# Edge indicators made by ScalarE, a bias added a stage earlier by VectorE, and VectorE's indicators one visit ahead, in a two-layer graph kernel

## What is computed

```python
h = relu(_layernorm(x))
# first layer (attention over edges, then a feed-forward part)
q, k, v = split(layernorm(h) @ Wqkv + bqkv)              # 8 heads of 32
e = exp(scores(q[src], k[dst]) - m[dst])
agg = segment_sum(v[src] * e / s[dst], dst)
x1 = h + agg
x = x + x1 + gelu(layernorm(x1) @ W_in + b_in) @ W_out + b_out
h = relu(_layernorm(x))
# second layer (8 relations from 4 bases)
W = einsum('rb,bio->rio', comp, basis)
msgs = einsum('ni,rio->nro', h, W)[src, edge_type]
z = gelu(segment_sum(msgs, dst) + h @ loop_w + h_bias + h)
x = x + layernorm(z) * ln_gamma + ln_beta
```

## Time and profile before

| | us |
|---|---|
| median of three runs | 1415.9 (1413.2 to 1416.32) |
| the profiled execution's own time | 1415.08 |
| its span, first to last instruction | 1413.4 |

### The profile page before, as it was taken

One profiled execution on the slowest core, in us unless ns is written; L12 is line 12 of the kernel. 1 busy time (PEld: TensorE's weight loads), 2 busy tenths in 40 slices (PEclk: granted clock), 3 DMA queues, 4 the chain that ended last, 5 costly groups with the idle time before them and its releaser, 6 DMA issues.

```text
span 1413.4 us, 18069 instructions
## 1 busy us (share of the span) xinstructions
PE 1154.9 (82%) x5223; PEld 829.5 (59%) x5223; DVE 895.7 (63%) x2778; ACT 453.0 (32%) x1150; POOL 995.6 (70%) x1032
## 2 busy tenths in 40 slices
PE   4875859999999999999999989677676767767674
PEld 2443647777777777777777765345454444444453
DVE  5664668888888888888888863124543454345345
ACT  4644215444544454445444533100000000000000
POOL 2755778788878877888788610577777777777773
PEclk9988979999999999999999999777878787788877
DMA  7758787888788878887888621344444444444442
GB/s 245 209 164 297 241 230 208 251 270 262 234 249 264 262 236 241 255 250 227 238 256 252 195 75 60 113 117 127 130 127 133 124 134 124 134 126 128 130 125 86
DMA packets 143355, 266.14 MB, mean 188 GB/s; under 512 B 41674, under 2 KB 89908, under 8 KB 140310
## 3 DMA queue, kind: packets, MB, share of 16 engines
q0 software_dynamic: 59536, 167.31, 41.5%
q1 hardware_dynamic: 82758, 96.47, 20.8%
q10 hardware_dynamic: 960, 1.18, 0.3%
HBM read 199.25 MB, written 65.63 MB: 187 GB/s over the span
## 4 chain that ended last, share of the span: by engine, by line
PE 33%; POOL 26%; DVE 18%; issue 11%; DMA 3%; ACT 0%; POOLq 0%; DVEq 0%; SPq 0%
POOL arena L1279 23%; PE ps L1520 8%; PE ps L1543 6%; PE ps L1551 6%; PE ps L1569 4%; DVE arena L1811 3%; PE ps L1509 3%; DVE arena L1809 3%; DVE arena L1744 2%; POOL arena L1225 2%; PE ps L1681 2%; DMA arena<-h_all,typs 1%; DVE arena L671 1%; PE ps L1489 1%; DVE arena L673 1%
## 5 line engine op out<-in xcount | busy, mean ns | idle before, releaser
L1225 POOL DMA_INDIRECT arena<-qv_tab,srcs x392 | 407.5, 1040 | 127.4 <-issue 115.9
L1279 POOL DMA_INDIRECT arena<-h_all,typs x392 | 381.7, 974 | 159.8 <-issue 117.3
L1681 PE MATMUL ps<-arena 128*128 128x256 f32 x784 | 279.6, 494 | 150.5 <-DMA arena<-h_all,typs 147.1
L1681 PEld LDWEIGHTS ps<-arena 128*128 128x128 f32 x784 | 169.4, 236 | 240.2 <-DMA arena<-h_all,typs 199.5
L1520 PE MATMUL ps<-arena 128*128 128x264 f32 x784 | 213.9, 401 | 30.6 <-DVE arena L1744 30.5
L1569 PE MATMUL ps<-wrel,arena 128*128 128x512 f32 x400 | 189.7, 600 | 2.4 <-ACT arena L1344 2.4
L1520 PEld LDWEIGHTS ps<-arena 128*128 128x128 f32 x784 | 139.1, 193 | 69.1 <-DVE arena L1744 43.9
L1744 DVE TENSOR_TENSOR arena<-arena 128x512 f32<-128x512 f32 x196 | 136.9, 699 | 40.8 <-ACT arena L1312 40.8
L1509 PE MATMUL ps<-arena 128*128 128x264 bf16 x1032 | 142.3, 279 | 11.2 <-DMA arena<-k_tab 11.2
L1509 PEld LDWEIGHTS ps<-arena 128*128 128x128 bf16 x1032 | 125.3, 144 | 44.6 <-issue 35.4
L1869 DVE TENSOR_TENSOR arena<-ps,rowb 128x256 f32<-128x256 f32 x25 | 10.6, 425 | 218.8 <-PE ps L1669 218.8
(11 more groups left out here) (164 smaller groups left out, 1474.6 us busy)
## 6 DMA issues: line engine op xcount, KB each, us to landing
h_all<-arena SPq DMA_DIRECT2D x23, 1024.0 KB, 5.5
arena<-dst SPq DMA_DIRECT2D x49, 256.0 KB, 5.1
rel<-arena SPq DMA_DIRECT2D x77, 128.0 KB, 2.2
arena<-k_tab SPq DMA_DIRECT2D x49, 198.0 KB, 4.1
att<-arena POOLq DMA_DIRECT2D x49, 132.0 KB
qv_tab<-arena SPq DMA_DIRECT2D x25, 256.0 KB, 3.1
arena<-qv_tab,srcs POOLq DMA_INDIRECT x392, 4.2
arena<-h_all,typs POOLq DMA_INDIRECT x392, 2.8
```

The source lines that it names most:

```text
L1225: pool.indirect_dma_start(out=rowbuf[:, 2 * q + t % 2, 0:2 * D], out_offset=None, in_=qv_tab, in_offset=bass.IndirectOffsetOnAxis(ap=srcs[ ...
L1279: pool.indirect_dma_start(out=rows1[:, u * T + t, :], out_offset=None, in_=h_all[0:N * R, :], in_offset=bass.IndirectOffsetOnAxis(ap=typs[ ...
L1681: last = nc.tensor.matmul(ps[:, 6 + u, 0:D], ind1[:, u, t, :], rows1[:, u * T + t, :], start=(t == 0), stop=(v == 0 and t == T - 1))
```

## The change

1. `b_out` is loaded behind the last x chunk. In stage 1 VectorE waits for it once, ahead of the block loop, and adds it to a block of x right after each `take(b)`. GpSimd's `residual` in stage 2 then has one addition.
2. TensorE's `turn` in stage 2 is gone. VectorE computes, once, the negative offset of each edge's `dst` from its window's start (`ndl`). ScalarE takes, for each tile, the square of (column number + that offset), and of four tiles at once Relu(1 - 2 * square), which is 1 where the two agree and 0 elsewhere. The Squares stand among ScalarE's other work, in two groups of four per visit.
3. The bank that the turns used becomes a second bank for the sums (`bank_a`), so a visit's first sum waits for the copy of the sums two visits back.
4. In stage 3 VectorE builds the indicators of visit v + 1 during visit v, between `combine` and `finish` of the block that the visit before ended. The copy of h (`h1c`) and the bank of `loop_part` get a second buffer.

```diff
@@ SP, stage 1
                 load_x(5)
+                sp.dma_start(rowb[:, 0, :], b_out.partition_broadcast(P)).then_inc(bias_in, 16)
...
-                    if 19 <= b < 23:
-                        sp.dma_start(rowb[:, b - 19, :], (b_out, h_bias, gamma, beta)[b - 19].partition_broadcast(P)).then_inc(s_w2, 16)
+                    if 19 <= b < 22:
+                        sp.dma_start(rowb[:, b - 18, :], (h_bias, gamma, beta)[b - 19].partition_broadcast(P)).then_inc(s_w2, 16)
@@ VectorE, stage 1
                 dve.wait_ge(s_w, 64)
+                dve.wait_ge(bias_in, 16)
                 for b in range(NBLK):
                     c, p = b // CH + 2, b % CH
                     more = b < NBLK - CH
                     take(b)
+                    nc.vector.tensor_tensor(x_block(xs, b), x_block(xs, b), rowb[:, 0, :], ALU.add)
@@ stage 2, banks
-            TURN, AGG = 4, 5
+            def bank_a(v):
+                return 4 + v % 2
@@ GpSimd, residual
-                    nc.gpsimd.tensor_tensor(x_of(m), x_of(m), h_of(m), ALU.add).then_inc(x_added, 1)
-                    pool.wait_ge(x_added, m + 1)
-                    nc.gpsimd.tensor_tensor(x_of(m), x_of(m), rowb[:, 0, :], ALU.add).then_inc(x_ready, 1)
+                    nc.gpsimd.tensor_tensor(x_of(m), x_of(m), h_of(m), ALU.add).then_inc(x_ready, 1)
@@ ScalarE, stage 2
-                def indicators(v):
-                    act.wait_ge(turn_ready, v + 1)
+                def distances(v, half):
                     if v >= 2:
                         act.wait_ge(agg_done, PAIRS * (v - 1))
-                    for half in range(2):
-                        nc.scalar.activation(ind[:, v % 2, 4 * half:4 * half + 4, :],
-                                             ps[:, TURN, half * 2 * WIN:(half + 1) * 2 * WIN].bitcast(BF16).rearrange("p (t w) -> p t w", w=WIN),
-                                             ACT.Copy).then_inc(ind_ready, 1)
+                    for t in range(4 * half, 4 * half + 4):
+                        last = nc.scalar.activation(ind[:, v % 2, t, :], iotaj[:, :], ACT.Square, bias=ndl[:, v, t:t + 1])
+                    last.then_inc(squares, 1)
+
+                def indicators(v, half):
+                    act.wait_ge(squares, 2 * v + half + 1)
+                    i = ind[:, v % 2, 4 * half:4 * half + 4, :]
+                    nc.scalar.activation(i, i, ACT.Relu, bias=ones[:, :], scale=-2.0).then_inc(ind_ready, 1)
@@ ScalarE, odd visits (even ones alike)
                         weights(v, 2)
+                        distances(v + 1, 0)
                         weights(v, 3)
+                        indicators(v + 1, 0)
                         if out:
                             keep_messages(out - 1, 2)
-                        indicators(v + 1)
+                        distances(v + 1, 1)
+                        indicators(v + 1, 1)
                         weights(v + 1, 0)
@@ TensorE, stage 2 (the three calls of turn are gone)
-                    if j == 0 and v >= 1:
-                        pe.wait_ge(osum_ready, v)
+                    if j == 0 and v >= 2:
+                        pe.wait_ge(osum_ready, v - 1)
                     for t in (2 * j, 2 * j + 1):
-                        last = nc.tensor.matmul(ps[:, AGG, 0:AW], ind[:, v % 2, t, :], rowbuf[:, 2 * ring(v, j) + t % 2, D:2 * D + H],
+                        last = nc.tensor.matmul(ps[:, bank_a(v), 0:AW], ind[:, v % 2, t, :], rowbuf[:, 2 * ring(v, j) + t % 2, D:2 * D + H],
@@ VectorE, stage 2, once
+                nc.vector.memset(ones, 1.0).then_inc(offsets_ready, 1)
+                nc.vector.tensor_tensor(ndl, wst[:, :].unsqueeze(2).broadcast_to([128, G, T]),
+                                        dstf[:, :].rearrange("p (g t) -> p g t", t=T), ALU.subtract).then_inc(offsets_ready, 1)
@@ VectorE, stage 3
+                indicators(0)
                 for v in range(G):
-                    m = block_of(v)
+                    ended = block_of(v - 1) if v else None
+                    if ended is not None:
+                        loop_sum(ended)
+                        combine(ended)
                     if v - 1 in EARLY:
                         loop_sum(EARLY[v - 1])
-                    if m is not None:
-                        copy_h1(m)
-                    indicators(v)
-                    if v % 2 and v > FIRST:
-                        loop_sum(block_of(v - 1))
-                        if v in EARLY:
-                            copy_h1(EARLY[v])
-                        combine(block_of(v - 1))
-                        finish(block_of(v - 1))
+                    if v + 1 < G:
+                        if loop_of(v + 1) is not None:
+                            copy_h1(loop_of(v + 1))
+                        indicators(v + 1)
+                    if ended is not None:
+                        finish(ended)
```

More of the change, by code:

```diff
@@ L725, in program @@
             zero = cut([D])
+            ndl = cut([G, T])
+            ones = cut([1])
             kg = cut([2, KW])
@@ L756, in bank_m @@
                 if m == LASTM - 1 and c >= 2:
-                    return (TURN, AGG)[c - 2]
+                    return (5, 4)[c - 2]
                 if m < LASTM:
@@ L1001, in program @@
             cut = carve()
-            h1c = cut([D])
+            h1c = cut([2, D])
             h1T1 = cut([2, P])
@@ L1367, in _ @@
                 diagonals(1)
-                indicators(0)
+                act.wait_ge(offsets_ready, 2)
+                for half in range(2):
+                    distances(0, half)
+                    indicators(0, half)
                 for v in range(G):
                     hid, out, old = hid_of(v), out_of(v), before(v)
+                    more = v + 1 < G
                     if v == FIRST:
-                        act.wait_ge(s_w2, 16 * 10)
+                        act.wait_ge(s_w2, 16 * 9)
                     if v == 0:
@@ L1398, in _ @@
                         keep_h1(old)
+                    if more:
+                        distances(v + 1, 0)
                     weights(v, 2)
+                    if more:
+                        indicators(v + 1, 0)
                     if old is not None:
@@ L1404, in _ @@
                     weights(v, 3)
-                    if v + 1 < G:
-                        indicators(v + 1)
+                    if more:
+                        distances(v + 1, 1)
+                        indicators(v + 1, 1)
                         weights(v + 1, 0)
@@ L1481, in _ @@
                         pe.wait_ge(special_over, 2)
-                def turn(v):
-                    if v >= 1:
-                        pe.wait_ge(ind_ready, 2 * v)
-                    tiles = indT[:, v % 2, :].rearrange("p (e t) -> p t e", t=T)
-                    for t in range(T):
-                        last = nc.tensor.transpose(ps[:, TURN, t * WIN // 2:(t + 1) * WIN // 2].bitcast(BF16),
-                                                   tiles[:, t, :], identb[:, :])
-                    last.then_inc(turn_ready, 1)
                 def keys(v, j):
@@ L1582, in _ @@
                 keys(0, 0)
-                turn(0)
                 keys(0, 1)
@@ L1588, in _ @@
                     if v == FIRST:
-                        pe.wait_ge(s_w2, 16 * 10)
+                        pe.wait_ge(s_w2, 16 * 9)
                     if v + 1 < BY_PE:
@@ L1599, in _ @@
                             message(out - 1, 2)
-                        turn(v + 1)
                         add_up(v, 2)
@@ L1631, in _ @@
                 penult, last = LASTM + 1, LASTM + 2
+                pe.wait_ge(osum_ready, G - 1)
                 message(LASTM - 1, 2)
@@ L1668, in loop_part @@
                     for k in range(2):
-                        last = nc.tensor.matmul(ps[0:P, 1, 0:D], h1T1[:, k, :], wloop[:, k, :],
+                        last = nc.tensor.matmul(ps[0:P, 1 + nth(m) % 2, 0:D], h1T1[:, k, :], wloop[:, k, :],
                                                 start=(k == 0), stop=(k == 1))
@@ L1863, in copy_h1 @@
                     dve.wait_ge(h1_kept, m + 1)
[L1864 removed]
+                    nc.vector.tensor_copy(h1c[:, nth(m) % 2, :], hs[:, m * D:(m + 1) * D]).then_inc(h1c_ready, 1)
                 def loop_sum(m):
@@ L1868, in loop_sum @@
                     dve.wait_ge(loop_psum, nth(m) + 1)
-                    own.did(nc.vector.tensor_tensor(h_m, ps[0:P, 1, 0:D], rowb[:, 1, :], ALU.add))
+                    own.did(nc.vector.tensor_tensor(h_m, ps[0:P, 1 + nth(m) % 2, 0:D], rowb[:, 1, :], ALU.add))
                     own.did(nc.vector.tensor_tensor(xs[:, m * D:(m + 1) * D], xs[:, m * D:(m + 1) * D], rowb[:, 3, :], ALU.add))
                     own.wait()
-                    own.did(nc.vector.tensor_tensor(h_m, h_m, h1c, ALU.add))
+                    own.did(nc.vector.tensor_tensor(h_m, h_m, h1c[:, nth(m) % 2, :], ALU.add))
                     own.wait()
```

13 lines of the change are left out of this document (6 added, 7 removed).

## The result

The change makes the kernel slower: 1450.62 us in the median of four runs (1449.04 to 1453.52) against 1416.11 us for four of before (1413.2 to 1418.82) on the same chip. The ratio is 1.0246, 95% interval 1.0220 to 1.0273. I had forecast 1423.5 us and a range up to 1430: the direction was right, the size was not. The profiled execution took 1451.25 us, its span is 1449.6 us, 36.2 more than before.

The account below looks back on a forecast made before the run. Stage 1 was taken as a chain of short steps, stage 2 as a TensorE-VectorE loop, stage 3 as GpSimd's gathers. 1415.08 - 0.6 + 5.1 + 3.7 + 0.4 - 0.6 = 1423.1, given as 1423.5; range 1408 to 1430.

Parts of the forecast that it names:

- The loop: Stage 2: 12.24 us of TensorE, 15.94 of VectorE and 0.08 of handover make the 28.26 us period, which stays within 0.1.
- Turns on the path: Rival, stage 2: TensorE decides, so removed turns shorten the period; 1413 us with one group, 1402 with both; chance 0.20.
- (a): Stage 2: TensorE's turns leave, but both groups stand outside the loop; -0.6 us, bounds 0 and -10.8, or -21.6.
- (b): ScalarE's indicators in stage 2: Squares and Relus are covered by ScalarE's waits; 0, bounds 0 and +33 us.
- table loads: Rival on ScalarE: Square changes the function table, two loads of 1283 ns per group of four; 1511 us, chance 0.04.
- (c): Stage 2: GpSimd's second residual addition leaves and the time turns into a longer wait; 0, bounds 0 and -25.5 us.
- (d): Second bank for the sums takes away a wait that no row of the middle periods shows; 0.
- (e): Stage 1: VectorE's bias additions, 15 on the path at 5.1 us, plus 3.7 for meeting GpSimd; bounds 0 and 12.6.
- (f): Stage 1: the first take waits for the bias load; 0.4 us with semaphore delay, bounds 0 and 1.5.
- Additions hidden: Rival, stage 1: waits for TensorE take up two thirds of the additions, GpSimd not met; 1416 us, chance 0.18.
- port term: Stage 1: additions reading two SBUF operands are slowed when they hit GpSimd's work; 3.7 us, 5.3 by the skill's rule.
- (g): End of stage 3: indicators built a visit earlier let the last sum follow the gathers; -0.6 us, bounds +0.5 and -1.2.

Follow-up runs that it names:

- with the turns kept: Kernel before with ScalarE's indicators; TensorE's turns stay, unread; bias part and third stage as before: 1424.04 us, ratio 1.0058.
- with the wait: Kernel before with ScalarE's indicators, turns kept unread, and GpSimd's residual additions waiting for VectorE's weighing of pair 2: 1420.53 us, ratio 1.0038.
- both waits: Changed kernel, eased stage 1; GpSimd's residual addition waits for pair 2's weighing, one gather for the next visit's comparison table: 1420.05 us, 1.0035.
- the bias part alone: Kernel before with b_out loaded ahead and added by VectorE in stage 1, one residual addition left on GpSimd, turns kept: 1440.72 us, ratio 1.0166.
- the eased stage 1: Changed kernel with b_out loaded behind the first stored block and stage 1's additions five blocks late, at the end of a block's work: 1434.39 us, 1.0140.
- the run with the additions one gather later: Changed kernel without the bias part, GpSimd's two residual additions moved behind the first gather of the next visit: 1425.31 us, ratio 1.0062.

## Why the prediction was wrong, step by step

**The loop** was read rightly: TensorE's 12.24 us did not change, the period never fell below 28.2, and L1530's wait for L1752 grew (forecast 0.5):

```profile
544.98 1.16 PE L1530 MATMUL ps<-arena 128*128 128x264 f32 x4 [0.95 <-DVE arena L1752]
```

"Turns on the path" is out.

**(a) Turns, -0.6.** Measured +9.6 us (643.0 with none, 633.4 with them kept; one profile each, and the second bank is in it). The step that failed is "both groups stand outside the loop", as an argument that nothing else hangs on them. TensorE's loop did not need them; but a sum behind one of them frees the ring, and so they set when GpSimd runs. I followed the removed work to the next wait of its own engine and not to those who wait for that engine.

**(b) ScalarE, 0.** Measured +8.7 us of stage 2 with the turns kept, +3.6 with the wait (628.3). The cover held as forecast: Squares are 388 ns in the median, their number of table loads did not grow (23 and 22 in stage 2, as before), and no Exp came late for the loop. With both waits and the same Squares and Relus stage 2 has 624.6, the length of before, so no cost of ScalarE's work in itself is shown. What the profiles with it have, and the three without it have not, are VectorE's short gaps, beside which the loop went into the other state. But those profiles also have two more VectorE instructions at the start of stage 2, and the profile names no cause for the gaps: it stays open.

**(c) Second residual addition leaves, 0 (0 to -25.5).** Alone it cost 6.6 us. This is the other failed step: "it is not the bound of stage 2, and the time turns into a longer wait". The wait did grow, to 71.4 us in the 20 periods from 260 to 830 of the changed kernel. But where GpSimd's remaining work lies in the period moved too, onto the weighing. In the bias part alone the ring's gather starts at 7.35 as before, and the addition comes at 15.72 instead of 16.78: it and two gathers behind it take 0.95, 1.06 and 0.95 us there and 1.19, 1.51 and 1.29 before. With the turns in place, either VectorE's instructions stretch GpSimd's gathers and the addition comes late, behind the weighing, or the gathers run undisturbed and it comes onto the weighing. Over all 14 profiles, 21 periods each, the weighing is stretched in all 132 periods in which the addition overlaps it and in none of the 162 others. Why the loop settles on the early side with one addition isn't shown; with both, and the turns kept, it was there in 15 of 21 periods. I had let the bounds end at no loss, with no reason that excluded one. With the turns gone no loss from the missing addition can be told: 638.7, 642.8 and 639.5 with one, 643.0 and 645.0 with two. The parts don't add up (9.6 + 8.7 + 6.6 = 24.9, measured 14.0) since they share one edge.

**(d) Second bank, 0.** Not run alone; no wait of the periods points to it.

**(e), (f) Stage 1, +9.2.** Measured +16.0: load and wait 5.6 (forecast 0.4, bound 1.5), additions 10.3 (8.8). Two terms were mis-sized. The load was issued at 16.47 us and not at 15.3, and landed 7.5 us later and not 6.3, so the first take came at 24.02 and not 21.7; in the four profiles with this load it comes at 23.40 to 24.39, in the others at 20.62 to 22.27. And the clock was missing from the sum: TensorE's busy time grew by 8.2 us, of which the change's share is open. "Additions hidden" is out for this place; five blocks later they were hidden. The port term of 3.7 us was nothing at all in the changed kernel, as the view of the additions' line shows (ns min/median/max):

```profile
L614 DVE TENSOR_TENSOR xs<-xs,rowb x25: 408/415/431, 25.0 to 133.0; 128x256 f32<-128x256 f32 x25
```

So the total for the additions came near with a wrong reason.

The Trainium skill's rule on the shared port (SBUF — State Buffer, SBUF: two separate sides) was weighed at the wrong place: of its estimate of 5.3 us for stage 1 these 431 ns show nothing, and it is stage 2 that shows the thing. In the eased stage 1 the same additions meet it too: they take 406 ns at least, 419 in the median and 1483 at most (L611). The longest starts at 76.23, 0.11 us behind an addition of GpSimd's (L335) that runs for 1.31 us; and yet that stage ends only 0.5 us later than before. That the later one waits out the earlier one agrees with that, and with 543.63 and 543.69: the weighing took 1.24 for 0.68 us, 0.56 of the 0.67 us for which the addition still ran. That a GpSimd operation with one SBUF tensor holds the port as well does not agree: in the changed kernel the addition at 36.39 takes 0.41 us inside a TENSOR_SCALAR of GpSimd (L330, from 35.50 for 1.57 us). That the earlier one runs undisturbed does not agree with the run with the bias part alone: there the weighing had started 0.34 us ahead and took 1.02 us, the addition 1.26.

**(g) End of stage 3, -0.6.** The last sum waits for a gather (0.83 us) and no longer for the indicators, as forecast. From the first gather to the end the old order took 520.4 to 522.3 us in five profiles and the new one 518.3 to 525.0 in nine: no effect that can be told.

## What to carry to other kernels

When an engine that is off the path gets less to do, or is released sooner, ask where in the period its work lands then: where two engines hinder each other, a move of half a microsecond can put it on the path. Follow removed work to those who wait for the engine, and give a freed engine bounds on both sides. Where the order between two engines matters for time, a wait on the other engine's event fixes it, and it costs nothing while the engine has time to spare.

## What was not expected of the hardware

- GpSimd's gathers stretch two short VectorE instructions too: the TENSOR_SCALAR of 128x8 from 0.16 to 0.42 us, that of 128x256 from 0.41 to 0.64, where no GpSimd arithmetic runs. One of 128x1 keeps its 0.15 us under a gather (at 540.28 in the changed kernel). With the gather 1.7 us later (8.53 instead of 6.80 into the period) the first is 0.16 again but for one period.
- The same program (turns kept, ScalarE's indicators) holds two steady periods, 28.27 and 28.7 us, and changes between them within one execution.
- The length of TensorE's idle stretch alone did not tell its clock. At the same place in stage 1, 3.28 us were followed by the lower level in the changed kernel and 1.63 by the higher one before (5.33 and 2.75 us for the same work); but 3.64 by the higher one in the run with the additions one gather later (2.75 us), and 2.00 by the lower one for the most part in the run with the turns kept (4.44 us).
